# A new table of steps for the work beside the attention scores, in both layers of a two-layer transformer block

## What is computed

```
xn = layernorm(x);  x = x + attn0(xn) + ffn0(xn)
xn = layernorm(x);  x = x + attn1(xn) + ffn1(xn)

attn0: 16 heads of width 8. q and k are RMS-normalized low-rank projections, each with a
       rotary-like second part; causal softmax(q k^T / sqrt(8)) v, then W_O per head
ffn0:  sigmoid(W_r mix_r(xn)) * (W_v relu(W_k mix_k(xn))^2), mix = with the token before
attn1: 16 heads of width 8; softmax(q k^T / sqrt(8) + phi_bias) v, then w_proj, b_proj
ffn1:  gelu(xn W1) W2; W1 and W2 are softmax-weighted sums of 32 low-rank products
```

## Time and profile before

| | |
|---|---|
| Median of 3 runs (lowest to highest) | 1690.92 us (1688.02 to 1692.27) |
| The profiled execution, its own time | 1698.63 us |
| Its span, first to last instruction | 1696.9 us |
| Mean granted TensorE clock, share of full | 0.979 |
| PE busy | 1487.6 us (88%) |
| DVE busy | 1367.7 us (81%) |
| ACT busy | 1250.4 us (74%) |
| POOL busy | 1036.8 us (61%) |

### The profile page before, as it was taken

One profiled execution on the slowest core, in us unless ns is written; L12 is line 12 of the kernel. 1 busy time (PEld: TensorE's weight loads), 2 busy tenths in 40 slices (PEclk: granted clock), 3 DMA queues, 4 the chain that ended last, 5 costly groups with the idle time before them and its releaser, 6 DMA issues.

```text
span 1696.9 us, 42089 instructions
## 1 busy us (share of the span) xinstructions
PE 1487.6 (88%) x16234; PEld 605.4 (36%) x16234; DVE 1367.7 (81%) x2493; ACT 1250.4 (74%) x2502; POOL 1036.8 (61%) x1369
## 2 busy tenths in 40 slices
PE   3779999999989999889889898999899988999895
PEld 2544444444444444432222232323232323232331
DVE  2177777788877778888799999989999899889891
ACT  1237777777777777776788888887888887888784
POOL 2346777777777777753555665566556655566555
PEclk9879999999999999998999999999999999999998
DMA  8323322332222323242222213322231222222200
GB/s 289 63 58 69 80 77 77 77 77 79 77 77 77 78 77 77 77 88 56 42 65 69 60 44 64 65 58 52 56 66 58 52 58 64 58 51 52 64 14 20
DMA packets 133159, 116.96 MB, mean 69 GB/s; under 512 B 16856, under 2 KB 125664, under 8 KB 132960
## 3 DMA queue, kind: packets, MB, share of 16 engines
q1 hardware_dynamic: 126272, 100.64, 24.8%
q0 software_dynamic: 4096, 8.40, 1.5%
q10 hardware_dynamic: 2592, 5.24, 0.9%
HBM read 79.63 MB, written 33.55 MB: 67 GB/s over the span
## 4 chain that ended last, share of the span: by engine, by line
PE 42%; ACT 16%; DVE 16%; POOL 14%; issue 6%; DMA 4%; SPq 2%; POOLq 0%; ACTq 0%; DVEq 0%
PE pv_acc L656 12%; ACT probs L979 10%; PE scores_transposed L672 9%; PE scores_transposed L594 8%; DVE maxs L1189 4%; POOL turn L1285 4%; PE scores_for_max L693 3%; DMA stacks<-parts_scratch 2%; PE scores_for_max L594 2%; POOL probs L1374 2%; DVE maxs L1192 2%; DVE big L1178 2%; DVE maxs L1216 2%; PE scores_transposed L765 2%; POOL msp L1359 1%
## 5 line engine op out<-in xcount | busy, mean ns | idle before, releaser
L979 ACT ACTIVATE probs<-scores_transposed 128x512 f32<-128x512 f32 x1664 | 903.7, 602 | 167.0 <-PE scores_transposed L672 154.0
L672 PE MATMUL scores_transposed<-stacks 62*128 62x512 bf16 (+3 forms) x2048 | 563.2, 343 | 51.0 <-ACT probs L979 24.5
L1374 POOL TENSOR_TENSOR probs<-probs,near_bias 128x512 f32<-128x512 f32 x256 | 329.8, 1291 | 340.1 <-ACT probs L979 337.8
L656 PE MATMUL pv_acc<-probs,vals 128*32 128x512 f32 (+3 forms) x4096 | 464.7, 525 | 6.3 <-POOL probs L1348 6.3
L1189 DVE TENSOR_REDUCE maxs<-scores_for_max 128x2 f32<-128x1024 f32 x325 | 390.3, 1219 | 58.4 <-PE scores_for_max L693 57.1
L672 PEld LDWEIGHTS scores_transposed<-stacks 62*128 62x128 bf16 x2048 | 155.7, 94 | 595.6 <-ACT probs L979 272.2
L693 PE MATMUL scores_for_max<-stacks 60*128 60x512 bf16 x1024 | 323.4, 386 | 35.6 <-DVE maxs L1189 28.4
L1192 DVE TENSOR_REDUCE maxs<-scores_for_max 128x1 f32<-128x512 f32 x374 | 244.6, 681 | 19.8 <-PE scores_for_max L693 17.5
L697 PE MATMUL scores_for_max<-stacks 60*128 60x512 bf16 (+3 forms) x1024 | 234.8, 305 | 8.9 <-DVE maxs L1220 3.9
L1220 DVE TENSOR_REDUCE maxs<-scores_for_max 128x1 f32<-128x512 f32 x256 | 174.8, 683 | 83.5 <-PE scores_for_max L709 83.4
L1348 POOL TENSOR_SCALAR_AFFINE_SELECT probs<-probs 128x512 f32<-128x512 f32 x256 | 160.9, 641 | 42.0 <-ACT probs L979 41.4
(11 more groups left out here) (135 smaller groups left out, 2035.0 us busy)
## 6 DMA issues: line engine op xcount, KB each, us to landing
stacks<-parts_scratch SPq DMA_DIRECT2D x768, 64.0 KB
parts_scratch<-parts SPq DMA_DIRECT2D x64, 384.0 KB, 2.6
x_tile<-in_L_attn_x_dram SPq DMA_DIRECT2D x16, 256.0 KB, 3.0
probs<-in_fc_B_dram ACTq DMA_DIRECT2D x1, 4096.0 KB, 21.4
stage_a<-in_fc_A_T_dram SPq DMA_DIRECT2D x1, 4096.0 KB, 16.6
stacks<-mT SPq DMA_DIRECT2D x256, 4.0 KB
x_res<-in_L_attn_x_dram SPq DMA_DIRECT2D x16, 256.0 KB, 3.4
x_tile<-x_between_layers SPq DMA_DIRECT2D x16, 256.0 KB
```

Source lines behind the costliest of these rows:

```text
L656: last = mm(acc[VW * j:VW * j + VW, q0:T], columns[:, first:first + VW], probs[:, row, column:column + width], start=(kt == 0 and pu % PAI ...
L672: last = mm(st[:, bank, column:column + T - q0], ks[p][rows, h, P * kt:P * kt + P], qs[p][rows, h, q0:T], start=True, stop=True)
L979: fn(probs[:, row, :], st[:, B.use(("st", u, number)).bank, :], ACT.Exp, scale=SCALE).then_inc(s["exp_done"], 1)
L1374: g.tensor_tensor(diag, diag, near_bias[:, kt, :].unsqueeze(1).broadcast_to([P, G, P]), ALU.mult).then_inc(s["emul_pool"], 1)
```

## The change

Only the two tables are changed: the order of the steps on each engine, not what is computed. In the first layer MT0 goes from slot 2 to 3, and PJ1 and OB are taken one slot later by ACT and DVE. In the second layer H0 goes from slot 3 to 1 (taken at 2), MT0 from 0 to 5, MT1 from 19 to 20, OA from 18 to 19, AT from 23 to 25, H3 from 27 to 26, Y0 from 53 to 52 (taken at once, not a slot later), Y2 and Y3 a slot earlier; NORM goes from 15 to 13, BESIDE from 24 to 21, STORE from 32 to 39, THIRD_Q from 36 to 41 and THIRD_K from 54 to 50.

```diff
--- before.py
+++ after.py
@@ -118,13 +118,13 @@
 
 
 WORK_USES = {
-    0: {"MT0": (2, 0, 0), "FR": (7, 0, 1), "FK": (8, 0, 1), "OA": (15, 1, -1), "MT1": (23, 0, 0),
-        "XT": (24, 0, 2), "PJ0": (27, 0, 2), "PJ1": (28, 0, 2), "MT2": (44, 0, 0), "FV": (43, 1, 1),
-        "OB": (46, 1, 0), "QT": (50, 0, 2), "MT3": (51, 0, 1), "KT": (54, 0, 2)},
-    1: {"H0": (3, 0, 1), "MT0": (0, 0, 0), "H1": (9, 0, 1), "H2": (16, 0, 1), "MT1": (19, 0, 0),
-        "OA": (18, 0, -1), "XT": (21, 0, 2), "AT": (23, 0, -1), "H3": (27, 0, 1), "PR": (30, 0, -1),
+    0: {"MT0": (3, 0, 0), "FR": (7, 0, 1), "FK": (8, 0, 1), "OA": (15, 1, -1), "MT1": (23, 0, 0),
+        "XT": (24, 0, 2), "PJ0": (27, 0, 2), "PJ1": (28, 1, 2), "MT2": (44, 0, 0), "FV": (43, 1, 1),
+        "OB": (46, 2, 0), "QT": (50, 0, 2), "MT3": (51, 0, 1), "KT": (54, 0, 2)},
+    1: {"H0": (1, 1, 1), "MT0": (5, 0, 0), "H1": (9, 0, 1), "H2": (16, 0, 1), "MT1": (20, 0, 0),
+        "OA": (19, 0, -1), "XT": (21, 0, 2), "AT": (25, 0, -1), "H3": (26, 0, 1), "PR": (30, 0, -1),
         "VP": (31, 0, 1), "QT": (34, 1, 2), "MT2": (40, 0, 0), "KT": (44, 1, 2), "OB": (48, 0, 0),
-        "Y0": (53, 1, 1), "Y1": (57, 0, 1), "MT3": (59, 0, 1), "Y2": (61, 0, 1), "Y3": (63, 0, 1)},
+        "Y0": (52, 0, 1), "Y1": (57, 0, 1), "MT3": (59, 0, 1), "Y2": (60, 0, 1), "Y3": (62, 0, 1)},
 }
 BY_DVE = ("OA", "OB", "FV", "QT", "KT", "PR")
 
@@ -135,8 +135,8 @@
         "SQUARE": (32, 2), "MEAN": (34, 2), "ROOT": (42, 2), "SCALE_QK": (47, 2), "POW": (10, 2),
         "SECOND_Q": (52, 2), "THIRD_Q": (52, 2), "SECOND_K": (57, 2), "THIRD_K": (60, 2), "KACT": (10, 1),
         "SCALE_K": (49, 2)},
-    1: {"LN": (0, 2), "NORM": (15, 2), "BESIDE": (24, -1), "STORE": (32, -1), "POW": (0, 2),
-        "SECOND_Q": (36, 2), "THIRD_Q": (36, 2), "SECOND_K": (46, 2), "THIRD_K": (54, 2)},
+    1: {"LN": (0, 2), "NORM": (13, 2), "BESIDE": (21, -1), "STORE": (39, -1), "POW": (0, 2),
+        "SECOND_Q": (36, 2), "THIRD_Q": (41, 2), "SECOND_K": (46, 2), "THIRD_K": (50, 2)},
 }
 def bf16_parts(x):
```

## The result

The changed kernel takes 1718.32 us (median of 4 runs, 1716.34 to 1724.45) against 1691.6 of the kernel before (now the median of 4 runs, 1688.02 to 1698.21): 1.0156 of its time, 95% interval 1.0125 to 1.0187. It is slower by 26.7 us, where 1697.0 was forecast with a range up to 1710. Its profiled execution took 1719.72 us with a span of 1718.0 us, 21.1 more than that of before, at a mean granted clock of 0.970 instead of 0.979.

A forecast was written before the change was run, and what follows sets the result against it. PE's order was taken to bound the first layer, DVE then PE the second, with the K load binding slot 32. First layer 0, second layer +0.45 a body, 13 x 0.45 = 5.9 us: 1690.9 + 5.9, about 1697 us; range 1680 to 1710.

The forecast's parts named there:

- The first layer's sum: First layer: gains and losses of moving MT0, PJ1 and OB sum to -0.1 to +0.1 us a body, about 0.
- a body that moves by more than 0.15 us: Sign against the prediction: the first layer's body moving by more than 0.15 us.
- KT's cover: First layer: PE's 0.61 us stall at KT absorbs OB's 0.6 us loss; without it OB would cost 8 us.
- MT0 in the first layer: MT0 one slot later: PE's 0.57 us wait for POOL goes, but the pv waits for a mask; gain 0.05.
- DVE's chain: Second layer, to the last pair of maxima before OA: DVE gets there 1.3 us earlier.
- the walked body: The second-layer body followed step by step in the prediction, its MT0 beginning at 1243.99.
- the 17.9 that had been named as a sign: Sign against the prediction: MT1 coming before 17.9 us in a second-layer body.
- The load: Second layer: the next stack's K half takes 10.8 us from first issue, so slot 32's scores wait for it.
- the case without lost races: The load binds, no race is lost: -0.3 + 0.2 = -0.1 us a second-layer body, 1689.5 us; chance 0.30.
- After slot 32: Second-layer stretch from slot 32 to the next MT0, 25.87 us, PE dense: change between -0.3 and +0.5 us.
- The races: H0's first and H1's second gelu step on DVE against POOL's multiplies: 1.85 us if lost, 0.55 taken on average.
- The rival for the slower side: Second layer: both races lost, +1.75 us a body, 1713 us; chance 0.13.

The follow-up runs named there:

- e2: The kernel before with only the first layer's OB taken two slots later instead of one: 1712.68 us, ratio 1.0085.
- e1: The changed kernel with the first layer's OB back, taken one slot later instead of two: 1710.69 us, ratio to before 1.0121.
- e6: The changed kernel with unread filler matmuls before the first layer's QT wait and the second layer's slot 32 wait: 1714.19 us, ratio 1.0124.
- e7: The changed kernel with MT1 and OA back in their old slots 19 and 18: 1693.27 us, ratio 0.9999.
- e3: The changed kernel with both halves of the next body's stack loaded behind MT0 in the second layer too: 1683.8 us, ratio 0.9943.
- e13: The changed kernel with OA alone back at slot 18, MT1 staying at 20: 1724.13 us, ratio 1.0183.
- e9: The changed kernel with OB back, both stack halves loaded behind MT0, and Y0, Y2 and Y3 back: 1661.23 us, ratio 0.982.
- e11: The kernel before with only MT1 and OA moved, to slots 20 and 19: 1719.7 us, ratio 1.0171.
- e5: The changed kernel with OB back and both stack halves loaded behind MT0 in the second layer: 1665.5 us, ratio 0.9836.
- e10: The kernel of e9 with MT1 and OA also back in their old slots: 1655.87 us, ratio 0.9772.

## Why the prediction was wrong

**The first layer's sum.** The step that failed reads: "That loss meets PE's next stall, 0.61 us at KT for POOL's sum, which does not move, and disappears in it", and from it "between -0.1 and +0.1 a body". As order and waits go it was right: the wait at KT vanished, and bodies without a fall of the clock take 42.04 to 42.18 us instead of 42.11. The new wait at slot 51 was 0.35 us, not 0.6. What the step left out is that a wait has a second price. Before, PE's waits of 1.05 and 0.61 us lay 2.6 us apart and the clock was 1.00; now 1.06 and 0.35 us lie 0.95 us apart, and in nine of thirteen bodies the clock is 0.5 behind them. e2 made that with OB alone, e1 undid it, e6 kept the waits and took away the fall. Waits and clock together are 1.13 us a body on average, 14.7 us in all, where a body that moves by more than 0.15 us had been named as a sign that the prediction is wrong. The prediction had priced the loss of KT's cover at 8 us and the clock at nothing, although it had read a mean clock of 0.979 and two regimes at 1.00.

**MT0 in the first layer.** "PE's wait of 0.57 us for POOL goes": 0.36 of it stayed, and the pv waits 0.28 us more for the mask. The pv stands at 1.93 us after slot 0, inside the forecast 1.9 to 2.0.

**DVE's chain, MT1 and the issue of the load.** Right to 0.1 us for the walked body. MT1 was put at 18.15 us (1261.1 in the walked body) and came at 18.12; the key half's first DMA was put at 20.2 and came at 20.21; 337 pairs and 350 single banks, as counted. Over the thirteen bodies MT1 comes at 17.7 to 18.3 us (in three of them before the 17.9 that had been named as a sign) and the first DMA at 19.8 to 20.4. Slot 20 comes 1.1 us earlier than before, 1.3 had been forecast for DVE there. One premise was wrong: "what DVE does is almost unchanged". DVE is busy for 1338.1 us instead of 1367.7, and its eight gelu steps sum to 5.8 us a body instead of 7.4. The difference comes from two steps that had met POOL in every body and no longer do, H0's second one ahead of slot 20 and, behind slot 20, H3's first one, which met BESIDE in the kernel before:

```profile
1269.44 1.28 POOL L1329 TENSOR_TENSOR x_res<-x_res,ffn 128x512 f32<-128x512 f32 x1
...
1270.12 1.15 DVE L1170 SCALAR_TENSOR_TENSOR fb<-fa,fd 128x512 f32<-128x512 f32 x1
```

H3's first step took 1.1 to 1.8 us before and 0.7 to 0.8 after. With the load as the last at slot 32, little of this was left there (0.17 us, next paragraph).

**The load.** The load had been taken at 10.8 us; it took 11.0 in the body shown, 10.2 to 12.0 in the thirteen, and 11.1 in the body of e7. The wait at slot 32 took the place of DVE in every body, as forecast, and slot 0 to 33 came out at 31.45 us against 31.62 before: -0.17, where the case without lost races had -0.3. e3 and e7 show that the load's end follows its issue, e7 and e13 together that the issue follows MT1. The fixed length holds for these twelve DMAs alone: in e3 the last of the 24 landed 12.8 to 24.1 us after the first issue.

**After slot 32.** "25.87 us to the next MT0, PE dense", with bounds of -0.3 to +0.5. Measured +1.00 a body: 0.70 in slot 33 to 48 and 0.30 in slot 48 to 0. The second is the three Y entries (e9), above the 0.1 to 0.2 that were taken. The first is the clock behind the wait for the load (e6, e3, e7 all have 11.28 or 11.29). The prediction had a wait of more than 1 us for the load at the price of its length.

**The races.** Of four bodies that differ in where the ring stands, one loses H0's first gelu step: 1.59 us at 1320.04, POOL having started 0.22 earlier; in the other POOL starts 0.03 later and its multiply takes 1.79 us. H1's second step is won in all. Before, the step of the earlier trace rows was lost in every body. The Trainium skill, SBUF — State Buffer, section "Who interferes with whom", calls the pair of ports that the two engines share an exclusive lock, on which the one that comes later waits. The trace agrees: the late steps are 0.9 and 0.5 us longer than the usual 0.68 and 1.27, where the other engine still had 1.0 and 0.65 us to run. The loss falls in one body of four, so the 0.55 us a body that the forecast took for both races was too much, and the case without a lost race was the nearer one up to slot 33.

**The sum again.** Without the clock: 0.09 us a body in the first layer, -0.17 + 0.30 in the second, 13 x 0.22 = 3 us, 1695 us, which is inside the forecast's 1692 to 1704, in part by luck: the 0.55 us that the forecast paid for the races was hardly spent, and the first layer and the Ys cost more than it had for them. The clock adds 13 x (1.04 + 0.70) = 23 us: 1717. The rival for the slower side was the wrong one: it had the races lost, at 1713 us.

**What stays open.** Why the same two waits are followed by a fall in nine first-layer bodies and not in the other four: PE's rows ahead of it agree to 0.01 us in the two bodies shown. It is no chance of a single run: in the changed kernel from the fifth body on, and in e3 through all thirteen, two bodies with a fall and one without follow each other. Nor does the length of the wait for the load decide alone: in the changed kernel the seven falls stand behind the seven longest waits, 1.58 to 2.44 us, but in e1 a wait as long was followed by none:

```profile
1563.61 0.39 PE L693 MATMUL scores_for_max<-stacks 60*128 60x512 bf16 x2 [2.42 <-DMA stacks<-parts_scratch]
...
1565.98 1.06 PE L656 MATMUL pv_acc<-probs,vals 128*32 128x512 f32 x8
```

Which entries besides MT0 win the second half of the 1.1 us in slot 0 to 20 was not tried.

## What to carry to other kernels

Where PE's granted clock is 1.00 and PE is close to the bound, price every new wait of PE twice: its length, and what the work behind it costs at the lower level; look at which other wait of PE stands next to it. A later stall may take up a new wait's length, as KT's did here, and the clock still falls. Before a step that other work hangs on is moved (here MT1, by one slot), follow what is queued behind it on the engine that it releases: here twelve DMAs that landed 10 to 12 us after their first issue, whenever that was. A new table is best tried entry by entry: here MT1 and OA (2.15 us a second-layer body) and the Ys (0.30) gave back more than the 1.6 us that the rest of the table had won, and OB in the first layer cost another 1.13.

## What the runs showed of the hardware

- The granted clock fell to 0.5 behind waits of PE that were short in themselves: 1.06 and 0.35 us in a first-layer body, 0.48 and 0.50 us in e11, 1.83 us at slot 32. It did not fall behind 1.05 and 0.61 us that lie 2.6 us apart, and behind the same rows it fell in nine bodies of thirteen, not in all. A pv of eight matmuls then took 1.44 to 1.94 us instead of 0.86 to 1.06, and the first-layer body 1.5 us more. Matmuls that nobody reads, in place of the idle time, kept it at 1.00 (e6). The Trainium skill, TensorE: Matmul & The Clock Gate, section "A second HAM failure mode: psum-queue depth-cycling", tells of a kernel in which frequent short pauses between groups of matmuls make the clock go back and forth between its two levels; the rows here agree with that.
- Twelve DMAs of 64 KB into eight partitions each took 11.0 and 11.1 us from first issue to last landing, whether they were issued at 18.3 or 20.2 us of the body; issued behind the other twelve, at 6.9 us, all 24 were in time in twelve of thirteen bodies in e3, in ten in e5 and in all in e9 and e10. In e3 the last of the 24 landed 12.8 to 24.1 us after the first issue.
